# A relational graph layer summed by one-hot products alone, with no gathered rows

## The reference

```python
edge_index = jnp.stack([src, dst])                 # src, dst sorted by dst
h = node_feat @ W_emb + b_emb
norm = _edge_norm(etype, dst, h.dtype)             # one number for each destination
for l in range(L):                                 # L = 2
    W = jnp.einsum('rb,bdf->rdf', w_coe[l], bases[l])   # 8 relations
    T = jnp.einsum('nd,rdf->rnf', h, W)
    msg = T[etype, src] * norm
    agg = jax.ops.segment_sum(msg, dst, num_segments=N)
    h = agg + h @ self_loop[l]
    h = bn_gamma[l] * (h - bn_mean[l]) * jax.lax.rsqrt(bn_var[l] + BN_EPS) + bn_beta[l]
    h = jax.nn.relu(h)
...
x = _layernorm(x + _L0_gnn_ref(...))
```

## Time and profile before

| | us |
|---|---|
| median of the runs timed | 7406.93 (7400.81 to 7423.84, 3 runs) |
| the profiled execution, its own time | 7325.07 |
| its span | 7323.3 |
| PE busy in the span | 4817.2 (66%) |
| DVE busy | 3736.0 (51%) |
| POOL busy | 2970.2 (41%) |
| ACT busy | 2254.1 (31%) |

### The profile page before, as it was taken

How to read it: one execution, slowest core, us unless ns; L and a number is a source line. 1 busy time by engine, 2 the same in 40 slices (tenths; PEclk the granted TensorE clock), 3 DMA queues, 4 the chain that set the end, 5 groups by cost and what they waited for, 6 DMA issues and landing times. The chain is left out here.

```text
span 7323.3 us, 142769 instructions
## 1 busy us (share of the span) xinstructions
PE 4817.2 (66%) x47884; PEld 3473.4 (47%) x47885; DVE 3736.0 (51%) x7626; ACT 2254.1 (31%) x3504; POOL 2970.2 (41%) x2606
## 2 busy tenths in 40 slices
PE   5466666666666566666664767766778846666778
PEld 2244444444444444444442444444444426666767
DVE  4254545554545454455453434433433169999943
ACT  2132323323323232333232322322321025555610
POOL 0444444444444444444422333333330017777700
PEclk8777777777777777778776877777779978887889
DMA  5444444444444444444443222222226634434368
GB/s 193 128 143 136 146 137 150 149 134 138 143 134 140 133 139 133 142 149 148 136 135 102 60 59 59 60 59 59 59 59 213 219 115 156 156 132 158 136 212 262
DMA packets 707511, 973.97 MB, mean 133 GB/s; under 512 B 173843, under 2 KB 590078, under 8 KB 700510
## 3 DMA queue, kind: packets, MB, share of 16 engines
q1 hardware_dynamic: 472418, 524.71, 22.7%
q10 hardware_dynamic: 160636, 295.81, 10.9%
q0 software_dynamic: 74368, 152.45, 8.4%
HBM read 665.78 MB, written 306.86 MB: 133 GB/s over the span
## 5 line engine op out<-in xcount | busy, mean ns | idle before, releaser
L650 POOL DMA_INDIRECT f_rows<-table,f_recs x1715 | 1648.4, 961 | 2028.4 <-DMA f_recs<-edge_records 1273.3
L770 PE MATMUL f_acc<-f_rows,f_hot 128*128 128x264 f32 x3430 | 1240.1, 527 | 363.8 <-issue 239.7
L770 PEld LDWEIGHTS f_acc<-f_rows,f_hot 128*128 128x128 f32 x3430 | 878.4, 267 | 593.1 <-issue 354.6
L1260 PE MATMUL g_zps<-g_ohot,g_grow 32*128 32x256 f16 x13464 | 635.0, 290 | 367.3 <-issue 366.3
L2089 POOL TENSOR_TENSOR a_weights<-a_powers,a_counts 128x896 f32<-128x896 f16 x245 | 724.3, 2962 | 329.5 <-ACT a_powers L2179 301.1
L2139 PE MATMUL a_psum<-state_and_spare,a_weights 128*128 (+1 forms) x4802 | 656.7, 307 | 299.5 <-POOL a_weights L2089 153.8
L1316 ACT ACTIVATE g_grow<-g_gps 128x512 f16<-128x512 f32 x825 | 452.4, 595 | 1146.6 <-DMA f_rows<-in_edge_attr 629.6
L2139 PEld LDWEIGHTS a_psum<-state_and_spare,a_weights 128*128 128x128 f32 x4802 | 646.0, 222 | 313.2 <-issue 211.2
L1355 DVE TENSOR_SCALAR g_ohot<-count,slot_target 128x256 f16<-128x256 f16 x1683 | 364.2, 285 | 841.1 <-DMA f_rows<-in_edge_attr 652.9
L1215 POOL DMA_INDIRECT g_rows<-table,g_recs x576 | 548.5, 952 | 574.0 <-DMA g_recs<-edge_records 407.8
L1035 DVE TENSOR_TENSOR state_and_spare<-f_count_up,f_key 128x2048 f16<-128x2048 f16 x196 | 349.8, 1785 | 713.0 <-PE f_cnt L712 373.6
(11 more groups left out here) (285 smaller groups left out, 6561.9 us busy)
## 6 DMA issues: line engine op xcount, KB each, us to landing
f_rows<-in_edge_attr SPq DMA_DIRECT2D x343, 320.0 KB
counts_by_destination_f<-f_counts_by_destination ACTq DMA_DIRECT2D x343, 224.0 KB
no_edge_penalty<-f_pen ACTq DMA_DIRECT2D x343, 224.0 KB
s_ring<-counts_by_destination_f SPq DMA_DIRECT2D x98, 784.0 KB
a_pen<-no_edge_penalty SPq DMA_DIRECT2D x49, 1568.0 KB, 10.0
a_counts<-counts_by_source_f SPq DMA_DIRECT2D x49, 1568.0 KB, 6.8
e_ring<-counts_by_source_f SPq DMA_DIRECT2D x343, 224.0 KB, 3.8
counts_by_source_f<-state_and_spare ACTq DMA_DIRECT2D x147, 512.0 KB
```

Source lines behind the costliest of these rows:

```text
L650: e.indirect_dma_start(out=rows[:, j, 0:D], out_offset=None, in_=k.table_d[0], in_offset=bass.IndirectOffsetOnAxis(ap=recs[:, j, 4:5].bitc ...
L770: m = e.matmul(acc[:, 0:GW], hot[:, j, :], rows[:, j, :], start=j == 0, stop=j == SLOTS - 1)
L1260: m = e.matmul(zps[:, u, 0:RELATIONS * QW], grow[s, gslot(b), i, q * D:(q + 1) * D], ohot[s, oslot(b), i, :], start=c == 0 and q == 0, sto ...
```

## The change

The second inner layer takes all 49 tiles by products. PE's loop has 48 passes of one tile each, and the last tile follows as straight code, as before. Everything of the way by messages goes: the record loads (`records`, L1163), POOL's 576 gathers (`messages`), DVE's one-hot matrices for them (`send`), PE's sums (`sum_messages`) and `close_half`. The bank that this frees is a third bank for the gather products (`GBANKS`), which go by pairs of cells as before. Since nothing reads `table_d[1]` in this path, the first inner layer no longer makes it: `table_rows`, ACT's copy and its transfers go, and the waits of `turn_counts` are turned to `t_sb` and `by_dst_moved`.

```diff
@@ phase_first: PE
             def turn_counts(t, g, final=False):
 
                 e.wait_ge(cnt_moved, t * (len(BLOCKS) * QUARTERS) + blocks_of(g) * QUARTERS)
-                if g < 2:
-                    e.wait_ge(table_sb, t * 2 + (g + 1))
-                elif g < len(FLIP_AT) or final:
+                if g == 0:
+                    e.wait_ge(t_sb, t + 1)
+                if g < len(FLIP_AT) or final:
                     e.wait_ge(by_dst_moved, t * NSEG + g)
...
-            def table_rows(t, half):
-
-                e.wait_ge(t_sb, t + 1)
-                e.wait_ge(by_dst_moved, t * NSEG + half)
-                e.matmul(pm[:, :], ht[:, :], k.wr[:, 1, half * (TW // 2):(half + 1) * (TW // 2)], start=True, stop=True)\
-                 .then_inc(table_ps, 1)
...
-                        if g in (3, 4):
-                            table_rows(t - 1, g - 3)
...
@@ phase_first: ACT
-                    if b in (1, 2):
-                        e.wait_ge(table_ps, t * 2 + b)
-                        e.wait_ge(table_out, (t * 2 + b - 1) * 16)
-                        e.activation(table[:, :], pm[:, :], ACT.Copy).then_inc(table_sb, 1)
-                        e.wait_ge(table_sb, t * 2 + b)
-                        e.dma_start(k.table_d[1][bass.ds(t * (P * RELATIONS), P * RELATIONS), :]
...
@@ phase_second
-        GBANKS = 2
+        GBANKS = 3
...
-                with e.Fori(0, UNITS - 1) as i:
-                    unit(i, False)
-                unit(UNITS - 1, True)
+                with e.Fori(0, NT - 1) as t:
+                    for i in range(SPIECES):
+                        e.wait_ge(s_made, t * SPIECES + (i + 1))
+                        piece(t + 1, i)
...
-                with e.Fori(0, 2 * UNITS) as n:
-                    messages(n, 0)
-                    leftover(n)
-                    messages(n, 1)
-                    messages(n, 2)
-                leftover(2 * UNITS)
...
@@ phase_second: PE
-                def tile(n, t, final):
+                def tile(t, final):
                     for b in range(1, NB):
                         for h in pairs(b):
-                            gather(n, t, h)
+                            gather(t, h)
                         for h in pairs(b - 1):
-                            scatter(n, h)
-                        if not final and b in SUM_AT:
-                            sum_messages(n, SUM_AT[b])
+                            scatter(t, h)
...
-                with e.Fori(0, 2 * UNITS) as n:
-                    tile(n, n + (n >> 1), False)
-                tile(2 * UNITS, NT - 1, True)
+                with e.Fori(0, NT - 1) as t:
+                    tile(t, False)
+                tile(NT - 1, True)
...
@@ phase_second: DVE
-                        if i is not None and b in SUM_AT:
-                            send(n, i, SUM_AT[b])
-                        targets(n, t, b, first)
-                        if b == 1 and not first:
-                            close_half(n - 1, *((i, 0) if v else (UNITS - 1 if i is None else i - 1, 1)))
+                        targets(t, b, first)
                         if b == OSLOTS - 2 and not first:
-                            close_products(n - 1, earlier)
+                            close(t - 1)
```

153 lines of the change are left out of this document (35 added, 118 removed).

## The result

The changed kernel took 6707.51 us (median of 4 executions, 6699.88 to 6730.79) against 7407.38 us for the kernel before (4 executions): ratio 0.9079, 95% interval 0.9049 to 0.9108. A later job, against fresh executions of before, gave 0.9105 (0.906 to 0.915). The forecast was 6800 us, range 6700 to 6930. One thing has to be said with this result: the experiments ran on five chips, and on one of them the kernel before took only 5497.27 us and a product-only second layer was slower than it.

What follows compares the result with a forecast made beforehand. The prediction took PE to be starved of instructions while POOL's indirect transfers run. From the profiled 7325 us it took 545 (second layer) and 60 (first layer), giving 6720, then added 82: 6802, said as 6800 us, range 6700 to 6930.

Steps and rivals of the forecast that it cites:

- The pace, step 1: Second inner layer: each product tile takes 22.1 us, from the clean tile's 21.83 us plus 0.27 us for register operations.
- the first tile, step 2: Second inner layer's first tile: without gathers and begun cold by PE, it takes 23 us, bounds 20 and 35.
- the second layer's 545 us: Second inner layer: last move of sums comes at 4979.3 instead of 5524.52 us, a gain of 545 us.
- The reading of the gaps: Both inner layers: PE is starved of instructions while POOL's indirect transfers run; slow stretch of 14.3 us behind a pass's start.
- The third bank: Second inner layer: a third bank for gather products lets nothing start earlier, counted at nothing.
- The first layer, 60 us: First inner layer: dropping `table_rows` gains 60 us, taken as half, between bounds of 0 and 130 us.
- the 82 us carried over: Whole kernel: the median of runs before lay 82 us above the profiled execution; this was added to 6720 us.
- Rival 1: Second inner layer: leftover's transfer or branch leaves a 1 to 3 us stall per pass, 48 to 144 us; chance 0.13.
- Rival 3: Second inner layer: the loop itself causes the slow stretch, 36.4 us a pass, some 80 us slower, 7490 us; chance 0.03.
- Rival 4: Second inner layer: a hidden second limit such as `srow` landing late, 5 us a tile, 240 us, so 7040; chance 0.05.

## Why the prediction was right

- *The pace, step 1: 22.1 us a tile, measured 21.89.* The tile behind the loop was the right control. The 0.27 us for register operations were too much; 0.06 are there. With *the first tile, step 2* (23 us, measured 3855.3 - 3832.9 = 22.4) this makes the second layer's 545 us into 555.7. POOL's first gather comes 11.8 us behind PE's first product, as in the kernel before (3844.72 and 3907.35). So what it waits for there is not the load of the records that the row of before names, which is gone, and it came in time for PE.
- *The reading of the gaps,* that POOL's gathers cause them, is shown for the chips that have the hold-up: without the gathers a pass is 26.2 us, and gathers put beside a product tile cost it 15.6 us. What I did not see is that it depends on the chip. No step and no rival of the prediction has this condition in it; that the change was timed where the hold-up is there is luck, and where it is not the product-only second layer is the slower one (1.036). The change removed 1629.0 - 868 = 761 us of hold-up (868 is 4725.2 - 3857.2, from the first product to the last move of sums without gathers) and added 205 us of products (1073.3 - 868); where there is no hold-up, only the loss is left.
- *The third bank:* nothing, as said.
- *The first layer, 60 us:* 62.6, and 58.0 on another chip, each between single executions. That a part and not the whole of the 130 us comes back holds, and its way shows: PE's idle time grew by 125 us, the "issue" ahead of the count products alone by 114.7. That it is half was a middle between 0 and 130, so that the number came out so near is partly luck; and on the chip without the hold-up it is nothing.
- *The mis-sized term is the last one of the sum, the 82 us carried over.* They turned out to be -2: the changed kernel's profiled execution took 6709.38 us, its median is 6707.51. The sum against the profiled execution, 6720, is 11 us off it, the forecast of 6800 is 92 us off the median. The 82 us were no constant of the launch: executions of before in one job lie between 7263.85 and 7331.39, and two profiled ones of the changed kernel, 66.4 us apart, differ by 54.2 us already at the second layer's first product (3832.9 and 3778.7), where the first layer's waits for "issue" ahead of the count products are 642.7 and 603.3 us. So much of the scatter lies in the first layer's hold-up; whether before's 82 us did is not shown.
- *Rival 1,* a stall left by the leftover's transfer, has a price of 0.0 us: 21.9 us a tile on the chip with the hold-up and on the one without. Only in the first tile, where it comes among scatter products and not at a tile's start, does a gap of 0.59 us follow it. It becomes real with company: three more gathers right behind it cost 1.5 us. *Rival 3,* the loop's own stretch (the prediction once calls it the last of its rivals), is out twice over: the scatter products have 0.6 us of "issue" in 49 tiles, and 26.2 us passes without gathers have the same branch. The rule that I had put against the forecast, in the Trainium skill's "Runtime: NRT & Kernel Launch", section "Instruction fetch mechanics", says that a taken branch makes an engine stand for its target page where that page is not among the two it holds; here 48 taken branches cost PE less than 1 us together, and whether their target lay outside those pages no row shows. *Rival 4,* `srow` late: DVE's waits gave PE no idle time but the 35.1 us at the layer's start.

What stays open is what the hold-up is. That it is a lack of supply to PE fits the rows (it waits for no counter, runs on for 45 to 58 products, gets a few at a time, and a pause refills it). But it is a reading: no row shows what an indirect transfer takes that a direct one of POOL doesn't, nor what differs on the chip without it. Nor do the transfers of instructions that the profile records show a refill. These are their queues in the kernel before from 3960 to 5460 us (packets, MB), 30 passes long:

```profile
q14 instruction: 4, 0.03, 0.0%
q8 instruction: 1, 0.02, 0.0%
```

A version better than both was not run. An estimate: gathers 2.9 us apart cost a tile 0.2 us for six, so 42 product tiles could carry 252 gathers, seven message tiles of 36; each spares 21.9 - 2 x 4.3 = 13.3 us of PE (a pass of before without gathers is 26.2 us, 4.3 more than a product tile, for half a message tile), 93 us, less 8 for the gathers. But messages need the table, and the table took 58 to 63 us in the first layer. So some 20 to 30 us would be left, on a chip with the hold-up.

## What to carry to other kernels

Where PE idles with "issue" as the releaser, look at what POOL does in that time: with indirect transfers in a row, a few are nearly free as long as they are over before PE has run its next 45 to 58 products (0.2 us for three in a row at a tile's start, but 3.7 for three among scatter products of 32 ns), and a long row costs PE about 1.3 us for each, whatever its size. So spacing them, or replacing them by products, is worth more than making them smaller. Judge such a trade on more than one chip: product-only plans stood at 0.91 to 0.92 where the hold-up was and at 1.036 where it wasn't. And make the sum against the profiled execution without adding its distance to the median, unless it is known to what that distance belongs.

## What was not expected of the hardware

- The same kernel took 5497.27 us on one chip and 7285.1 to 7407.38 us in the five other measurements, four of them known to be from other chips. The difference lies in the phases with indirect transfers: the first layer's end (2824.2 against 3895.5 us) and the pass (26.2 against 49.7 us). POOL's own pace is the same in both, a gather each 1.25 us.
- An indirect gather holds PE's supply by the instruction (37.1 to 37.7 us a tile for 12, with 128 or 16 rows, of 512 or 64 bytes); 24 direct transfers from the same engine not at all (21.9 us).
- A gather each 2.9 us is nearly free (22.1 us a tile with six), one each 1.25 us costs 8.0 us for six.
- PE runs on for 45 to 58 products behind the first gather, which is 1.74 us among scatter products and 4.6 us at a tile's start.
- Ahead of an indirect transfer that follows another one, two empty instructions of POOL make the gap 2.4 us instead of 0.30; twelve semaphore instructions mostly make it 0.44.
- POOL clearing a buffer takes a DVE instruction of 285 ns to 586 ns, and the tile from 21.9 to 28.1 us.
